# A router in packed float32r products, its logits turned by VectorE and moved by small transfers, and outputs added by transfer

## The chip, the cores and the metric

One core of a Trainium2 chip runs the kernel. The metric is the device time of one execution in microseconds (us). The core's engines work side by side, each through its own queue in order: TensorE (PE; its weight loads are listed as PEld), VectorE (DVE), ScalarE (ACT), GpSimd (POOL) and SyncE (SP), which issues transfers. Queues meet only at semaphores, counters that one instruction raises and another waits for.

## The reference

`x` has 8 x 2048 rows of 256 numbers. It is computed, in float32:

- x = x + attention(layernorm(x)): Q, K, V from 64 x 256 weights, energy = K^T V over each sequence, context = Q energy, out = context Wo^T, all without softmax
- x = x + ffn(layernorm(x)), with h the normalised row:

```
scores = sigmoid(h @ Wr)                      # 8 experts
idx = top 2 of scores + router_bias           # weights are normalised over the two
routed = sum over the 4 MLP experts of cw * (silu(h Wg) * (h Wu)) Wd
       + cw[4] h + cw[6] h + cw[7] relu(h)    # expert 5 gives nothing
shared = causal depthwise convolution of h over 4 rows, plus bias
ffn = routed + shared
```

## The kernel before, in words

The 16384 rows are cut into 32 groups of 512 rows (`GT`, four tiles of 128). The loop runs in steps; in each step every stage works on another group, by the lags of L34: I loads x, L normalises (first layernorm), A transposes it and gathers K^T V, Q projects, X loads x a second time into `acc`, B adds the attention and normalises again, R routes, C runs experts and convolution, Y finishes and stores. A head (`head` of each engine) does groups up to step 7, then `steps(body)` runs steps 7 to 39. The order of each engine's instructions is written out by hand in its `body`. Every fourth step is a chain step (`chain()`): a new sequence starts and the 64 x 64 energy is worked out in short dependent steps. Steps without stage A that are no chain step are drain steps (`drain()`).

Exact products are made from halves: a float32 value is split into a rounded float32r part (`_hi`) and the rest (`_lo`), and three float32r products stand for one (`three`, L408). PE's eight PSUM banks are `ps_gram`, `ps_gu0` to `ps_gu2`, `ps_y0`, `ps_y1`, `ps_sh0`, `ps_sh1`. `ps_sh` holds in turn the transposes of x2 (`x2_transpose`), the router's logits, the attention output, the transposed expert weights and the transposes of xn (`xn_transpose`).

What the change touches, by engine:

- PE, `router` (L535): eight float32 products of a 128 x 128 tile of `x2T` with 128 x 8 router weights, giving logits with token rows on partitions. It waits for the copies `x2T` and for the first `x2T_low`. `weights_transpose` (L593) turns the 128 x 16 expert weights `cw` into `ps_sh1`.
- ACT: `logits_copy` (L867) takes logits and their absolute values out of PSUM, `score_size` and `score_dip` (L888, L894) go on with them, `weights_copy` (L911) takes the transposed weights out.
- DVE: `route_scores` and `route_weights` (L1138, L1160) find the two experts and the weights `cw`; `residual` and `norm2_stats` (L1095, L1103) follow in the queue; `output` (L1215) adds the finished `ps_y` onto `acc`, in two passes; `norm1_stats` (L1083) has a one-element copy (`turn`) between its two parts as a wait.
- POOL: `gate_weight` (L1386) multiplies the gate by the expert weights spread over all partitions (`cwb`); `relu_add` (L1399) is an adding transfer from `x2` to `acc`; `norm2_factors` (L1407) makes scale and shift of the second layernorm for ACT's `norm2` (L834).
- SP, `spread_weights` (L348): stores `cwT` to memory, waits for it, and loads it back four times, spread over the partitions. `body` (L377) has the order load x, store outputs, spread weights, load `acc`.

`gate_up(st, k)` (L414) is a group of six 512-column products, k = 0 to 7; `down(st, stage, e)` (L435) one of twelve 256-column products, e = 0 to 3; `conv_transpose` (L448) puts the convolution into `ps_y`.

## Time and profile before

| what | us |
|---|---|
| median of three runs (lowest, highest) | 886.65 (884.33, 886.78) |
| the profiled execution's own time | 888.19 |
| its span, first to last instruction | 886.4 |
| PE busy in the span | 852.9 (96%) |
| DVE, ACT, POOL busy | 751.2, 643.2, 409.6 |
| mean granted TensorE clock, share of full | 0.988 |

Busy time of PE is modelled up to the end of each product, and products overlap, so the distance between two starts, not the duration, is what a product costs the queue. An idle time stands in brackets with the instruction that ended it. The 1.8 us between span and time lie outside the instructions.

### The profile page before, as it was taken

What the parts mean: (1) busy time and instruction counts of PE and PEld (TensorE: products, weight loads), DVE (VectorE), ACT (ScalarE), POOL (GpSimd) and SP (SyncE); (2) the same over time, 40 slices, a digit from 0 to 9 for tenths busy, and PEclk for the clock granted to TensorE, in tenths of its full rate; (3) what the DMA queues carried; (4) which work ended last, traced back from release to release, by engine and by line L of the source; (5) the groups of instructions that cost most, each with busy time, mean ns of one, the idle gap of its engine ahead of it and who ended that gap; (6) DMA issues with size and microseconds to landing.
All of it is one profiled execution on the core that took longest, in us unless ns stands there. A gap on an engine that the chain in (4) does not pass through costs nothing.

```text
span 886.4 us, 16852 instructions
## 1 busy us (share of the span) xinstructions
PE 852.9 (96%) x5437; PEld 757.1 (85%) x5437; DVE 751.2 (85%) x2093; ACT 643.2 (73%) x1366; POOL 409.6 (46%) x585
## 2 busy tenths in 40 slices
PE   5878999999999999999999999999999999899997
PEld 4667888999889988889899998889988998788886
DVE  4668889988899988999899998999889988678884
ACT  4585867787777777787678777777867875666653
POOL 3214635554455454455355544545535544433332
PEclk9899999999999999999999999999999999999999
DMA  9112354433354442434443344554424344324434
GB/s 286 60 43 54 119 144 138 112 110 100 116 143 143 143 120 67 126 125 138 143 121 104 100 132 120 143 144 126 111 75 131 109 121 119 96 54 118 118 94 119
DMA packets 79447, 103.86 MB, mean 117 GB/s; under 512 B 6528, under 2 KB 58880, under 8 KB 79360
## 3 DMA queue, kind: packets, MB, share of 16 engines
q1 hardware_dynamic: 74752, 86.02, 30.6%
q0 software_dynamic: 4608, 16.78, 10.0%
q8 instruction: 43, 0.70, 0.3%
q14 instruction: 44, 0.36, 0.1%
HBM read 68.96 MB, written 17.04 MB: 97 GB/s over the span
## 4 chain that ended last, share of the span: by engine, by line
PE 77%; DVE 12%; ACT 4%; issue 3%; POOL 2%; DMA 1%; POOLq 0%; DVEq 0%; ACTq 0%
PE ps_gu L410 11%; PE ps_gu L412 10%; PE ps_gu L411 10%; PE ps_sh L541 6%; PE ps_y L410 6%; PE ps_y L411 6%; PE ps_y L412 6%; PE ps_y L460 3%; PE ps_sh L531 3%; PE ps_sh L484 2%; ACT x L842 2%; PE ps_sh L588 1%; PE ps_sh L589 1%; PE ps_gram L618 1%; PE ps_gu L564 1%
## 5 line engine op out<-in xcount | busy, mean ns | idle before, releaser
L1391 POOL TENSOR_TENSOR gate<-gate,cwb 128x512 f32<-128x512 f32 x128 | 168.0, 1313 | 291.4 <-ACT gate L765 265.6
L410 PE MATMUL ps_gu<-x2T_hi,wgu_hi 128*128 128x512 f32 x512 | 211.3, 413 | 1.2 <-DVE hid L1055 1.2
L412 PE MATMUL ps_gu<-x2T_hi,wgu_lo 128*128 128x512 f32 x512 | 202.2, 395 | 0.0
L411 PE MATMUL ps_gu<-x2T_lo,wgu_hi 128*128 128x512 f32 x512 | 201.7, 394 | 0.0
L410 PE MATMUL ps_y<-wd_hi,hid_hi 128*128 128x256 f32 x512 | 153.1, 299 | 2.2 <-DVE hid_lo L1062 2.2
L1073 DVE SCALAR_TENSOR_TENSOR conv<-x2T,conv_w,conv 128x512 f32<-128x512 f32 x192 | 150.6, 822 | 0.0
L411 PE MATMUL ps_y<-wd_lo,hid_hi 128*128 128x256 f32 x512 | 145.4, 284 | 0.0
L412 PE MATMUL ps_y<-wd_hi,hid_lo 128*128 128x256 f32 x512 | 145.0, 283 | 0.0
L1062 DVE TENSOR_TENSOR hid_lo<-hid,hid_hi 128x512 fp32r<-128x512 f32 x101 | 86.2, 853 | 46.2 <-ACT hid_hi L758 46.2
L412 PEld LDWEIGHTS ps_gu<-x2T_hi,wgu_lo 128*128 128x128 f32 x512 | 96.6, 189 | 22.2
L410 PEld LDWEIGHTS ps_gu<-x2T_hi,wgu_hi 128*128 128x128 f32 x512 | 97.2, 190 | 18.4 <-issue 2.3
L411 PEld LDWEIGHTS ps_gu<-x2T_lo,wgu_hi 128*128 128x128 f32 x512 | 97.4, 190 | 13.4
L1055 DVE TENSOR_TENSOR hid<-ps_gu,gate 128x512 f32<-128x512 f32 x128 | 86.2, 673 | 20.8 <-issue 13.3
L410 PEld LDWEIGHTS ps_y<-wd_hi,hid_hi 128*128 128x128 f32 x512 | 97.9, 191 | 4.9 <-DVE hid_lo L1062 3.5
L765 ACT ACTIVATE gate<-ps_gu 128x512 f32<-128x512 f32 x128 | 75.5, 590 | 33.5 <-PE ps_gu L412 32.7
L411 PEld LDWEIGHTS ps_y<-wd_lo,hid_hi 128*128 128x128 f32 x512 | 98.0, 191 | 1.6
L412 PEld LDWEIGHTS ps_y<-wd_hi,hid_lo 128*128 128x128 f32 x512 | 97.5, 190 | 0.0
L758 ACT ACTIVATE hid_hi<-hid 128x512 fp32r<-128x512 f32 x128 | 80.2, 626 | 18.5 <-DVE hid L1055 17.6
L1370 POOL TENSOR_TENSOR mv<-mv,eps_ln 128x4 f32<-128x4 f32 x64 | 24.3, 380 | 136.9 <-DVE mv L1112 114.0
L826 ACT ACTIVATE xn<-xa,shift,rstd 128x256 f32<-128x256 f32 x128 | 66.0, 591 | 6.5 <-POOL shift L1375 6.4
L1373 POOL TENSOR_TENSOR rstd<-mv,half_neg 128x4 f32<-128x4 f32 x64 | 67.4, 1054 | 5.0
L842 ACT ACTIVATE x<-acc,shift,rstd 128x256 f32<-128x256 f32 x128 | 66.3, 593 | 4.3 <-POOL shift L1375 4.2
(126 smaller groups left out, 1877.5 us busy)
## 6 DMA issues: line engine op xcount, KB each, us to landing
cwb<-cw_rows SPq DMA_DIRECT2D x128, 256.0 KB, 4.0
xa<-in_x SPq DMA_DIRECT2D x32, 512.0 KB, 7.8
acc<-in_x SPq DMA_DIRECT2D x32, 512.0 KB, 6.9
acc<-x POOLq DMA_DIRECT2D x32, 512.0 KB, 4.6
out<-acc SPq DMA_DIRECT2D x64, 256.0 KB, 2.6
cwb<-in_wg SPq DMA_DIRECT2D x4, 128.0 KB, 3.9
cwb<-in_wu SPq DMA_DIRECT2D x4, 128.0 KB, 3.7
cwb<-in_wd SPq DMA_DIRECT2D x1, 512.0 KB, 4.5
```

The costliest lines, as they stand in the source:

```text
L410: nc.tensor.matmul(dst, a_hi, b_hi, start=start, stop=False, skip_group_check=True)
L411: nc.tensor.matmul(dst, a_hi, b_lo, start=False, stop=False, skip_group_check=True)
L412: return nc.tensor.matmul(dst, a_lo, b_hi, start=False, stop=stop, skip_group_check=True)
L758: return nc.scalar.activation(dst, src, ACT.Copy, scale=scale)
L765: nc.scalar.activation(gate[:, e % 2], ps_gu[GU_BANK[2 * e]][:, :], ACT.Silu)\
L826: nc.scalar.activation(xn[:, q, t], xa[:, q, t], ACT.Identity, bias=shift1[:, f, t:t + 1], scale=rstd1[:, f, t:t + 1]).then_inc(xn_ready, 1)
L842: nc.scalar.activation(x2[:, q, t], acc[:, st.slot("B", 4), t], ACT.Identity, bias=shift2[:, q, t:t + 1], scale=rstd2[:, q, t:t + 1]).then ...
L1055: v.tensor_tensor(hid[:, e % 2], ps_gu[GU_BANK[2 * e + 1]][:, :], gate[:, e % 2], ALU.mult)\
L1062: v.tensor_tensor(hid_lo[:, k], hid[:, k], hid_hi[:, k].bitcast(F32), ALU.subtract)\
L1073: v.scalar_tensor_tensor(conv[:, c], x2T[:, q, c, k:k + GT], conv_w[:, c, k:k + 1], conv[:, c], ALU.mult, ALU.add).then_inc(conv_ready, 1)
L1373: g.tensor_tensor(rstd, mv[:, :, 1], half_neg[:, :], ALU.pow).then_inc(rstd_ready, 1)
L1391: g.tensor_tensor(gate[:, e % 2], gate[:, e % 2], cwb[:, q, e], ALU.mult).then_inc(gatew_ready, 1)
```

## The change

PE's router becomes four products: the weights are held as 8 columns of high halves, 8 of low halves and 16 of zeros (`wr2`, 128 x 32, float32r), the tokens move past them as 512 columns of `x2T_hi` and then of `x2T_lo`. The logits come out with tokens along the free axis on 32 partitions. DVE turns them in 32 x 32 blocks, POOL adds the two halves of each logit, SP moves them in four transfers to token rows, and ACT takes the absolute value from SBUF. The weights `cw` are turned by DVE instead of PE and ACT, and stored by four transfers. In steps with both Y and C that are no drain steps, ACT copies `ps_y` to `y_rows` and POOL adds it onto `acc` by a transfer. The one-element copy in the first layernorm's statistics goes in the loop. In the head the first group's convolution taps move ahead of the loop; in the last chain step the residual and its statistics go ahead of the routing. The diff, cut to its core:

```diff
+    def by_transfer(self):
+
+        return self.on("Y") and self.on("C") and not self.drain()
...
 # SP
+            def move_logits(st):
+
+                sp.wait_ge(sum_ready, st.before("R", 1, 1))
+                if st.later("R", 1):
+                    sp.wait_ge(cw_ready, st.before("R"))
+                for j in range(P // SQ):
+                    sp.dma_start(logits[j * SQ:(j + 1) * SQ, :], summed[:, j].rearrange("p t e -> p (t e)"))\
+                        .then_inc(logits_loaded, 16)
...
             def spread_weights(st):
-                sp.dma_start(rows.rearrange("a e (t n) -> (a e t) n", t=TG), cwT[:, :]).then_inc(cw_stored, 16)
-                sp.wait_ge(cw_stored, st.before("R", 16, 16))
+                for j in range(P // SQ):
+                    sp.dma_start(rows[:, :, :].rearrange("a e (t n) -> (a e t) n", t=TG)[:, j * SQ:(j + 1) * SQ],
+                                 cwT[j * SQ:j * SQ + EM * TG, :]).then_inc(cw_stored, 16)
+                sp.wait_ge(cw_stored, st.before("R", 64, 64))
...
             def body(st):
                 if st.on("I"):
                     load_x(st)
+                if st.on("R"):
+                    move_logits(st)
                 if st.on("Y"):
...
+                    if st.by_transfer():
+                        sp.wait_ge(y_added, st.before("Y", 16, 16))
...
 # PE: xn_transpose(1) and x2_transpose(1) no longer wait for cwT_ready
             def router(st):
-                pe.wait_ge(x2T_ready, st.before("R", HC, HC))
+                b, q = ps_sh[0][0:SQ, :], st.slot("R", 2)
                 pe.wait_ge(x2Tlo_ready, st.before("R", HC, 1))
-                b, q = ps_sh[0], st.slot("R", 2)
-                for t in range(TG):
-                    for c in range(HC):
-                        last = nc.tensor.matmul(b[:, t * NE:(t + 1) * NE],
-                                                x2T[:, q, c, PAD + t * P:PAD + (t + 1) * P], wr_sb[:, c],
-                                                start=(c == 0), stop=(c == HC - 1))
+                pe.wait_ge(x2Thi_ready, st.before("R", HC, HC))
+                for c in range(HC):
+                    nc.tensor.matmul(b, wr2[:, c], x2T_hi[:, q, c], start=(c == 0), stop=False,
+                                     skip_group_check=True)
+                for c in range(HC):
+                    if c == 1:
+                        pe.wait_ge(x2Tlo_ready, st.before("R", HC, HC))
+                    last = nc.tensor.matmul(b, wr2[:, c], x2T_lo[:, q, c], start=False, stop=(c == HC - 1),
+                                            skip_group_check=True)
                 last.then_inc(router_done, 1)
...
-            def weights_transpose(st):
...
 # ACT
+            def y_copy(st, h):
+
+                if h == 0:
+                    act.wait_ge(y_done, st.before("Y", 1, 1))
+                else:
+                    act.wait_ge(down_done, st.before("Y", EM, EM))
+                if st.later("Y", 1):
+                    act.wait_ge(y_added, st.before("Y", 16))
+                copy(y_rows[:, 2 * h:2 * h + 2].rearrange("p t n -> p (t n)"), ps_y[h][:, :]).then_inc(out_ready, 1)
...
-            def logits_copy(st):
...
             def score_size(st):
-                act.wait_ge(logits_ready, st.before("R", 2, 2))
+                act.wait_ge(logits_loaded, st.before("R", 64, 64))
                 if st.later("R", 1):
                     act.wait_ge(cw_ready, st.before("R"))
+                nc.scalar.activation(size[:, :], logits[:, :], ACT.Abs).then_inc(size_ready, 1)
+                act.wait_ge(size_ready, st.before("R", 1, 1))
...
-            def weights_copy(st):
...
             def head():
                 q_high(at("Q", 1, NG))
-                logits_copy(r)
-                score_size(r)
-                score_dip(r)
                 xnT_head(3, 0)
                 xnT_head(3, 1)
                 q_high(at("Q", 2, NG))
+                score_size(r)
+                score_dip(r)
                 norm1(at("L", 6, NG))
...
             def body(st):   # y_copy(0) follows x2T_out(0), y_copy(1) follows x2T_out(1)
...
                         nc.scalar.activation(a, a, ACT.Identity, bias=skip_bias[:, q, t:t + 1],
                                              scale=skip_scale[:, q, t:t + 1]).then_inc(ident_added, 1)
+                if r_on:
+                    score_size(st)
+                    score_dip(st)
...
 # DVE
+                dve.wait_ge(cw_ready, st.before("R", 1, 1))
+                if st.later("R", 1):
+                    dve.wait_ge(cw_stored, st.before("R", 64))
+                v.transpose(cwT[:, :], cw[:, q].rearrange("p e t -> p (e t)")).then_inc(cwT_ready, 1)
+
+            def logits_turn(st):
+                dve.wait_ge(router_done, st.before("R", 1, 1))
+                if st.later("R", 1):
+                    dve.wait_ge(sum_ready, st.before("R"))
+                v.transpose(turned[:, :, :, :].rearrange("p j t n -> p t j n"),
+                            ps_sh[0][0:SQ, :].rearrange("p (t j n) -> p t j n", t=TG, j=P // SQ))\
+                    .then_inc(turn_ready, 1)
...
                 q_low(at("Q", 3, NG))
+                dve.wait_ge(halo_ready, 1)
+                conv_tap(at("C", 0, NG), 0)
+                conv_tap(at("C", 0, NG), 1, (0,))
                 q_low(at("Q", 4, NG))
                 xnT_low(at("A", 5, NG), 0)
                 xnT_low(at("A", 5, NG), 1)
+                conv_tap(at("C", 0, NG), 1, (1,))
+                conv_tap(at("C", 0, NG), 2, (0,))
...
-                if y_on:
+                if y_on and not st.by_transfer():
                     output(st, 0)
                     output(st, 1)
...
+                if c_on and not first:
+                    hidden(st, 0)
+                if r_on:
+                    logits_turn(st)
+                if c_on and not first:
                     conv_tap(st, 2)
...
                     hidden(st, 2)
+                if b_on and m_on and not st.on("A"):
+                    residual(st, 0)
+                    residual(st, 1)
+                    norm2_stats(st)
                 if r_on:
                     route_scores(st)
...
 # POOL
+            def y_add(st):
+
+                k = st.slot("Y", 4)
+                pool.wait_ge(relu_added[st.slot("Y", 2)], st.uses("Y", 2, 16, 16))
+                pool.wait_ge(out_ready, st.before("Y", 2, 2))
+                g.dma_start(acc[:, k].rearrange("p t n -> p (t n)"), y_rows[:, :, :].rearrange("p t n -> p (t n)"),
+                            accum_op=ALU.add).then_inc(y_added, 16)
...
+            def logits_sum(st):
+
+                pool.wait_ge(turn_ready, st.before("R", 1, 1))
+                if st.later("R", 1):
+                    pool.wait_ge(logits_loaded, st.before("R", 64))
+                g.tensor_tensor(summed[:, :, :, :].rearrange("p j t e -> p (j t) e"),
+                                turned[:, :, :, 0:NE].rearrange("p j t e -> p (j t) e"),
+                                turned[:, :, :, NE:2 * NE].rearrange("p j t e -> p (j t) e"), ALU.add)\
+                    .then_inc(sum_ready, 1)
...
                 norm2_factors(at("B", 1, NG))
+                logits_sum(at("R", 0, NG))
...
                     gate_weight(st, 1)
+                if r_on:
+                    logits_sum(st)
+                if st.by_transfer():
+                    y_add(st)
                 if c_on:
                     gate_weight(st, 2)
```

## Rows read from the trace of the kernel before

**Rows 1.** Windows: us; busy us of PE, PEld, DVE, ACT, POOL; clock; DMA.

```profile
124.37:749.15 624.78, 623.97 (x4082) 558.88 (x4081) 559.68 (x1549) 480.54 (x1023) 316.46 (x428) 1.00 0.42 120
404.27:429.39 25.12, 25.12 (x166) 22.78 (x165) 22.81 (x66) 19.65 (x42) 13.35 (x19) 1.00 0.43 127
429.39:458.30 28.91, 28.87 (x189) 25.21 (x188) 25.26 (x68) 21.50 (x49) 13.19 (x19) 1.00 0.38 114
```

**Rows 2.** Timeline of PE around one router: start us, duration us, engine, line.

```profile
409.15 1.84 PE L541 MATMUL ps_sh<-wr_sb,x2T 128*128 128x8 f32 x16
410.86 0.48 PE L410 MATMUL ps_gu<-x2T_hi,wgu_hi 128*128 128x512 f32 x1
411.18 0.39 PE L411 MATMUL ps_gu<-x2T_lo,wgu_hi 128*128 128x512 f32 x1
411.41 0.39 PE L412 MATMUL ps_gu<-x2T_hi,wgu_lo 128*128 128x512 f32 x1
```

**Rows 3.** Timeline of PE at the transpose of the expert weights.

```profile
425.40 0.27 PE L600 MATMUL ps_sh<-ident,cw 128*16 128x128 f32 x1
425.51 0.60 PE L484 MATMUL ps_sh<-ident,xn 128*128 128x128 f32 x4
```

**Rows 4.** Timelines: the round from x2's transposes to the next x2.

```profile
405.46 0.60 PE L531 MATMUL ps_sh<-ident,x 128*128 128x128 f32 x4
417.64 0.40 PE L412 MATMUL ps_gu<-x2T_hi,wgu_lo 128*128 128x512 f32 x1
418.13 0.69 DVE L1055 TENSOR_TENSOR hid<-ps_gu,gate 128x512 f32<-128x512 f32 x1 [0.51 <-issue]
422.50 0.22 DVE L1179 TENSOR_TENSOR cw<-raw,winv 128x32 f32<-128x32 f32 x1
428.11 0.20 POOL L1375 TENSOR_TENSOR shift<-negm,rstd 128x4 f32<-128x4 f32 x1
428.64 2.07 ACT L842 ACTIVATE x<-acc,shift,rstd 128x256 f32<-128x256 f32 x4
```

**Rows 5.** Timelines: what stands before and behind the router.

```profile
409.34 0.67 DVE L1186 TENSOR_TENSOR x2T_lo<-ps_sh,x2T_hi 128x512 fp32r<-128x512 f32 x1
407.96 0.60 ACT L758 ACTIVATE x2T<-ps_sh 128x512 f32<-128x512 f32 x1 [0.78 <-PE ps_sh L531]
413.70 1.03 PE L460 MATMUL ps_y<-ident,conv 128*128 128x128 f32 x8
414.91 2.07 ACT L1005 ACTIVATE acc<-acc,skip_bias,skip_scale 128x256 f32<-128x256 f32 x4
```

**Rows 6.** Group (busy us, mean ns, idle before); transfers (KB, us to landing); SP's timeline.

```profile
L1186 DVE TENSOR_TENSOR x2T_lo<-ps_sh,x2T_hi 128x512 fp32r<-128x512 f32 x64 | 42.9, 671 | 15.0 <-ACT x2T_hi L758 14.3
cw_rows<-cwT SPq DMA_DIRECT2D x32, 8.0 KB, 1.4
acc<-x POOLq DMA_DIRECT2D x32, 512.0 KB, 4.6
acc<-in_x SPq DMA_DIRECT2D x32, 512.0 KB, 6.9
400.88 0.33 SPq L353 DMA_DIRECT2D cw_rows<-cwT  x1
```

**Rows 7.** Timelines of DVE and POOL where both work on SBUF at once.

```profile
415.05 1.44 DVE L1062 TENSOR_TENSOR hid_lo<-hid,hid_hi 128x512 fp32r<-128x512 f32 x1 [0.72 <-ACT hid_hi L758]
414.64 1.30 POOL L1391 TENSOR_TENSOR gate<-gate,cwb 128x512 f32<-128x512 f32 x1 [3.27 <-ACT gate L765]
```

**Rows 8.** Timelines of the head, the first expert step and the first drain step.

```profile
52.33 2.08 ACT L826 ACTIVATE xn<-xa,shift,rstd 128x256 f32<-128x256 f32 x4
53.53 0.20 POOL L1375 TENSOR_TENSOR shift<-negm,rstd 128x4 f32<-128x4 f32 x1
74.69 1.62 PE L460 MATMUL ps_y<-ident,conv 128*128 128x128 f32 x8 [2.91 <-DVE conv L1073]
771.66 1.86 PE L531 MATMUL ps_sh<-ident,x 128*128 128x128 f32 x4 [2.16 <-ACT x L842]
```

More of the change, by code:

```diff
@@ L398, in _ @@
             load_x(at("I", 7, NG))
+            move_logits(at("R", 0, NG))
             spread_weights(at("R", 0, NG))
@@ L740, in body @@
                     gram_halves(st)
-                if drain:
-                    down(st, "C", 2)
-                if r_on:
-                    weights_transpose(st)
                 if a_on and r_on:
                     xn_transpose(st, 0)
-                if c_on and not drain:
+                if c_on:
                     down(st, "C", 2)
@@ L865, in f_copy @@
                            [(f1[:, :], ps_gram[:, 0:H]), (f2[0:D, :], ps_gram[0:D, 0:H])], fhi_out)
-            def logits_copy(st):
-                act.wait_ge(router_done, st.before("R", 1, 1))
-                if st.later("R", 1):
-                    act.wait_ge(cw_ready, st.before("R"))
-                copy(logits[:, :], ps_sh[0][:, 0:TG * NE]).then_inc(logits_ready, 1)
-                nc.scalar.activation(size[:, :], ps_sh[0][:, 0:TG * NE], ACT.Abs).then_inc(logits_ready, 1)
             def halo(st):
@@ L909, in conv_begin @@
                         .then_inc(tap_ready, 1)
-            def weights_copy(st):
-                act.wait_ge(cwT_done, st.before("R", 1, 1))
-                if st.later("R", 1):
-                    act.wait_ge(cw_stored, st.before("R", 16))
-                copy(cwT[:, :], ps_sh[1][0:EM * TG, 0:P]).then_inc(cwT_ready, 1)
             def xnT_head(n, c):
@@ L974, in body @@
                     x2T_out(st, 0)
+                if st.by_transfer():
+                    y_copy(st, 0)
                 if m_on:
@@ L978, in body @@
                     x2T_out(st, 1)
+                if st.by_transfer():
+                    y_copy(st, 1)
                 if m_on:
@@ L1019, in body @@
                     norm1(st)
-                if r_on:
-                    weights_copy(st)
-                if st.on("B") and st.drain():
+                if st.on("B") and not st.on("A"):
                     norm2(st)
@@ L1031, in body @@
                     xnT_high(st, 1)
-                if st.on("B") and not st.drain():
+                if st.on("B") and st.on("A"):
                     norm2(st)
@@ L1060, in hid_low @@
                 dve.wait_ge(hidhi_ready, st.before("C", EM, e + 1))
+                if e == 0 and st.on("L") and not st.later("C", 1):
+                    dve.wait_ge(stat1, st.before("L", TG, TG))
                 k = e % 2
@@ L1063, in hid_low, with conv_tap @@
                     .then_inc(hidlo_ready[k], 1)
-            def conv_tap(st, n):
+            def conv_tap(st, n, parts=range(HC)):
                 q, k = st.slot("C", 2), PAD - 1 - n
-                for c in range(HC):
+                for c in parts:
                     if n == 0:
@@ L1090, in norm1_stats, with norm1_aggr, norm1_both @@
                     v.bn_stats(stats1[:, f, t], xa[:, q, t]).then_inc(stat1, 1)
-                turn(stat1, st.before("L", TG, TG))
+            def norm1_aggr(st):
+                f = st.slot("L", 2)
                 for t in range(TG):
                     v.bn_aggr(mv1[:, f, t], stats1[:, f, t]).then_inc(aggr1, 1)
+            def norm1_both(st):
+                norm1_stats(st)
+                turn(stat1, st.before("L", TG, TG))
+                norm1_aggr(st)
             def residual(st, h):
@@ L1185, in x2T_low @@
                 dve.wait_ge(x2Thi_ready, st.before("R", HC, c + 1))
+                if c == 0 and st.on("L") and st.later("C", 1):
+                    dve.wait_ge(stat1, st.before("L", TG, TG))
                 v.tensor_tensor(x2T_lo[:, q, c], ps_sh[c][:, :], x2T_hi[:, q, c].bitcast(F32), ALU.subtract)\
@@ L1267, in head @@
                 q_low(at("Q", 1, NG))
+                logits_turn(r)
                 residual(at("B", 1, NG), 0)
@@ L1329, in body @@
                     hid_low(st, 2)
-                if b_on and not drain:
+                if b_on and st.on("A"):
                     residual(st, 0)
```

99 lines of the change are left out of this document (53 added, 46 removed).

## The prediction

> **What bounds the kernel now.** I read the windows first, then PE's timeline in one step, then the other engines' timelines beside it. In the six rounds of four steps between the chain steps' routers, PE is busy 623.97 of 624.78 us at granted clock 1.00, that is at 2.4 GHz [rows 1]. A plain step takes 25.12 us with PE busy in all of it, DVE in 22.81, ACT in 19.65; the longer window of a chain step, 28.91 us, is as full [rows 1]. Busy time of PE is modelled, so I looked at starts: 512-column products of one kind start 0.23 us apart with nothing between [rows 2]. PE's queue is therefore the price list: what leaves it shortens the step until another wait ends last.
>
> The next limit is near. The round from one x2 to the next is closed: x2_transpose(0) at 405.46, gate_up(5)'s last product ends at 417.64 + 0.40 = 418.04, DVE's hidden(2) starts at 418.13, the routing gives cw at 422.50, then residual and statistics, POOL's shift is ready at 428.31, ACT's pass over x2 runs from 428.64 to 430.71 [rows 4]. PE comes to the next x2_transpose(0) one step of 25.12 [rows 1] after 405.46, at 430.58: it starts before the last of four ACT passes has ended. No slack is left there.
>
> **Router (PE).** From its start at 409.15 to the next group's at 410.86 it takes 1.71 us. The first product after it needs 0.32 us instead of 0.23 [rows 2]; I charge the 0.09 to the change from float32 to float32r. Removed: 1.80. Added: four float32r products of 512 columns. The trace has none with a 128 x 32 weight tile; the nearest rows, with 128 x 128, stand 0.23 apart, and I take that, since a smaller tile has less to load: 4 x 0.23 = 0.92. The dear end is 4 x 0.32 = 1.28. Net: -0.88, at worst -0.52. The fourth product waits for x2T_low(1), which ended at 410.01 [rows 5]; PE would be there at 409.15 + 0.69 = 409.84. With 0.35 us won ahead of it on DVE (the statistics' second half moves behind x2T_low(0), the one-element copy goes) the wait is 0 to 0.2 us.
>
> **Weights' transpose (PE).** Its slot runs from 425.40 to 425.51 [rows 3]: -0.11. ACT loses the copy behind it and the waits of xn_transpose(1) go. Together PE alone would save 0.99 us per step: 24.13 instead of 25.12.
>
> **DVE.** Two output passes on a PSUM bank go, 2 x 0.67 by [rows 6], x2T_low, the nearest pass of that size; logits_turn comes, 32 x 512 from PSUM, between 0.22 (cw, 128 x 32 [rows 4]) and the port-slowed 1.44 [rows 7]; I take 0.67, since the free size is the same 512. cw's transpose costs a wait of 0.1 and about 0.2 by the cw row, 0.3 in all, at most 0.67. The sum is -0.4, but the 0.3 lies on the closed round and the output passes did not. That round becomes 12.58 (405.46 to 418.04) - 0.88 + 0.09 + 12.58 (418.13 to 430.71) + 0.3 - 0.2 - 0.13 = 24.34. The 0.2 is ACT's: its pass began 0.33 after POOL's shift because its queue was full, and the lost copy and an earlier q_high free it. The 0.13 is the overlap of PE's first transposes with the last pass. So the step is 24.34, and PE waits about 0.2 us in it: **-0.8 per step**. x2's ACT pass is what is late next.
>
> **ACT.** The copies of ps_y are 2 x 0.60. The first fits the 0.78 us for which ACT waits between the two x2T_out [rows 5]; the second pushes silu(1), gate_weight(1) and hidden(1) by some 0.3, which DVE does not notice as its queue is behind. Without that gap, up to 1.2 us of 5.47 idle (25.12 - 19.65) go. conv_transpose waits for y_copy instead of output, and y_copy is earlier.
>
> **POOL and SP.** logits_sum stands ahead of gate_weight(2), and y_add too; the cover is the 3.27 us for which POOL waits there [rows 7]. The sum costs 0.20 (128x4, [rows 4]) to 1.30 (128x512, [rows 7]), taken 0.5, since 128 elements a lane are nearer to 4; y_add costs an issue. Its landing takes 4.6 us [rows 6]. SP waits for it ahead of the store of cw, which comes only after the routing, about 12 us later: covered. On SP, move_logits issues four transfers ahead of the outputs and spread_weights three more stores; at 0.33 each [rows 6] that is 1.3 us each time. The store of this step was issued at 400.88 + 25.12 = 426.00 [rows 1, 6], 3.3 after cw was there at 422.72, since PE's and ACT's part lay between; now it begins at 423.0, and the last of four at 424.0, so the spread weights come some 2 us sooner.
>
> **Do the logits arrive in time?** In the step of [rows 5]: router ends 410.2, hidden(0), turn to 411.4, sum to 411.9, four issues to 413.2, landing 1.4 [rows 6] after the last issue began: 414.3. ACT asks for them after its skip passes, 416.98 less the step's 0.8 [rows 5]: slack 1.9. DVE needs the result at 418.7, and ACT's three small passes end some 0.8 after the skip: about 1 us of further slack.
>
> **Steady part.** 25 router intervals from step 8 to 33 x 0.8 = 20.0 us. Chain steps are as full of PE [rows 1] and have the same router and round; I use the same 0.8.
>
> **Head.** logits_sum stands behind norm2_factors, whose shift is ready at 53.73 [rows 8]. Sum 0.5, issues 1.3, landing 1.4: 56.9, the three small passes to 57.7. ACT's queue holds norm1 behind them, which started at 52.33 [rows 8]: 5.3 late, and everything up to step 7's x2_transpose hangs on ACT there; cw's transpose adds 0.3. Gained: the 2.91 us that PE waited for the convolution taps, and the slower products after it (eight transposes 1.62 against 1.03 [rows 5, 8], the twelve of down(0) by about 1.0, an estimate in the same ratio): 1.6. Net **+1.0**, between -3 and +4.
>
> **End.** In the last chain step the residual moves ahead of the routing: of the 2.16 us wait [rows 8] and the slow products after it most goes, but hid_low(2) now stands behind more: -2.5, between 0 and -4. Three drain steps at -0.8: -2.4. The last store of cw has no cover; it loses PE's and ACT's part and gains three issues: 0.
>
> **Sum:** -20.0 + 1.0 - 2.5 - 2.4 = -23.9. The profiled execution took 888.19 with a span of 886.4; it would be 864.3 with 862.5. The median, 1.54 lower, would be about **863**.
>
> **The rivals.**
>
> A, the gain is given back at the port of DVE and POOL. While POOL's gate ran, DVE's hid_low took 1.44 us [rows 7] instead of 0.67 as x2T_low [rows 6]. logits_sum falls on conv_tap(2), and conv_transpose (413.70 [rows 5]) would come at 413.0 with the taps done at 412.6: 0.4 of slack. A sum of 1.30 instead of 0.5, or y_add's issue held back, costs 0.4 to 0.8 a step: half of the gain goes, 25 x 0.4 = 10 more, 873; at 0.8 all of the steady gain, 883. For it: DVE's and POOL's like overlaps are in every step. Against: the sum is small. The Trainium skill (SBUF — State Buffer, SBUF: two separate sides) says that such a pair of operations takes the shared port by turns, the loser waiting for the whole instruction; the 1.44 agrees. By that rule alone one sum costs DVE no more than its own 0.5, 0.1 beyond the slack: 25 x 0.1 = 2.5, near 865.
>
> B, slower: the logits are late. Place: ACT's score_size, in front of relu, conv_begin, silu(3). Price: every us past the slacks goes into the step. With landing L, a step changes by -0.8 + max(0, L - 1.4 - 2.4), my 2.4 lying between ACT's 1.9 and DVE's 2.9; it is slower from 4.6 on. At 6.9, the landing of acc<-in_x [rows 6], +2.3: 25 x 2.3 = 58, with head and end (-3.9) about 940. At 5.0 it is +0.4, 893. Against it: that row moves 512 KB, these 4 KB in a transfer, and the small store's is 1.4.
>
> C, the change doesn't do what it says: the 32-wide product costs more than a 128-wide one, or other waits than PE's end the step. Then the router stays at 1.3 to 1.8 us, the step gains 0 to 0.4, and with head and end the time is 873 to 883.
>
> **How the numbers follow.** Forecast (PE-bound or nearly, -0.6 to -0.99 a step) 0.70, A 0.14, B 0.06, C 0.10. About 0.3%, 2.7 us, is what a measurement of this kernel can tell from no change. Of A and C, 0.04 lies within that; B is slower but for the cases below 4.6, and I add 0.01 for a head that is stuck longer. Faster 0.89, same 0.04, slower 0.07. The forecast's own range: -0.99 x 28 and the good ends of head and end (-3, -4) give 852; -0.6 x 28 with +4 and 0 give 874. The range that holds 8 in 10 is **852 to 876**: it takes in A's nearer half and C's best, and leaves out the rest of A and C, and B.
>
> **What would show it.** The router's four products at 0.23 us spacing, 24.2 to 24.5 us from router to router in plain steps, no PE slot between gram_halves and xn_transpose; PE's waits, some 0.2 us a step, put down to ACT's x pass. DVE's turn at 0.6 to 0.7 us, POOL's sum under 0.7, ACT's abs without a wait for the transfer. In the head ACT idle for some 4 us ahead of the abs, but no wait of PE for conv taps in step 7. Wrong would be: PE waiting for conv, hid_lo or q in each plain step; ACT waiting for the logits in the loop; router products 0.3 us apart or more; DVE without any idle time in a step; or a head longer by over 4 us.

## The result: 930.6 us, 5% slower

The changed kernel took 930.62 us (median of 4 runs, 930.25 to 931.7) against 885.49 for the kernel before in the same runs: ratio 1.0499, 95% interval 1.0478 to 1.0521. The forecast was 863, range 852 to 876. The profiled execution has a span of 928.8 us, 42.4 more than before.

The page's first line, then two windows (us; busy us of PE, PEld, DVE, ACT, POOL; clock; DMA share; GB/s): one plain step, and the same six rounds of four steps as in [rows 1], from chain router to chain router:

```profile
PE 839.3 (90%) x5021; PEld 709.6 (76%) x5021; DVE 760.8 (82%) x2081; ACT 661.4 (71%) x1355; POOL 487.0 (52%) x644
```

```profile
404.27:430.95 26.68, 24.80 (x152) 21.12 (x152) 23.80 (x66) 20.43 (x41) 16.35 (x21) 1.00 0.55 139
129.01:791.47 662.46, 616.43 (x3770) 524.45 (x3768) 566.52 (x1526) 499.05 (x1023) 384.38 (x476) 0.99 0.52 133
```

A plain step takes 26.68 us instead of 25.12, and PE, busy in all of it before, now has idle time, 1.9 us in the step and 46.0 us in the six rounds (0.8 before). From the first router to the last the trace is 42.10 us longer: the two intervals at the head +3.43 (forecast +1.0), the next 25 together +38.98 (691.20 against 652.22), which is 1.56 each (forecast -20.0), the last chain step -1.63 (forecast -2.5), the three drains +1.32 (forecast -2.4). TensorE's clock is a small part of it: three chain intervals hold a stretch of 3.4 us at granted clock 0.50 and take 30.99, 31.19 and 31.83 us, the two next to them without one 30.91 and 30.80, so some 1.5 us in all.

Four of the rows on what waits for what in the whole changed kernel (us in total, times, longest):

```profile
ACT size L911 <- DMA logits<-summed: 58.8, 27, 5.4
PE ps_sh L515 <- DVE acc L1121: 35.2, 23, 3.2
DVE rmag L1162 <- ACT mag L913: 27.7, 20, 2.8
PEld ps_sh L574 <- DVE x2T_lo L1219: 18.9, 23, 1.5
```

The first row is a wait that the kernel before cannot have, as ACT copied the logits from PSUM itself. One plain step, by the engines' timelines (start us, duration us, engine, line, operation, tiles, in brackets the idle time before and who ended it):

```profile
404.87 0.70 DVE L1210 STREAM_TRANSPOSE turned<-ps_sh 32x512 f32<-32x512 f32 x1
405.50 1.36 DVE L1086 SCALAR_TENSOR_TENSOR conv<-x2T,conv_w,conv 128x512 f32<-128x512 f32 x2
406.79 0.67 DVE L1075 TENSOR_TENSOR hid_lo<-hid,hid_hi 128x512 fp32r<-128x512 f32 x1
...
411.83 0.69 DVE L1066 TENSOR_TENSOR hid<-ps_gu,gate 128x512 f32<-128x512 f32 x1 [0.15 <-issue]
413.52 0.35 DVE L1162 RECIPROCAL rmag<-mag 128x32 f32<-128x32 f32 x1 [1.00 <-ACT mag L913]
...
417.21 0.21 DVE L1204 STREAM_TRANSPOSE cwT<-cw 128x32 f32<-128x32 f32 x1
417.80 1.43 DVE L1075 TENSOR_TENSOR hid_lo<-hid,hid_hi 128x512 fp32r<-128x512 f32 x1 [0.38 <-ACT hid_hi L773]
```

```profile
405.65 2.14 POOL L1488 TENSOR_TENSOR summed<-turned 32x128 f32<-32x128 f32 x1 [0.15 <-DVE turned L1210]
407.74 0.92 POOL L1470 DMA_DIRECT2D acc<-y_rows  x1
...
417.39 1.29 POOL L1449 TENSOR_TENSOR gate<-gate,cwb 128x512 f32<-128x512 f32 x1 [4.28 <-ACT gate L780]
```

```profile
407.81 3.33 SPq L368 DMA_DIRECT2D logits<-summed  x4
...
417.45 1.72 SPq L377 DMA_DIRECT2D cw_rows<-cwT  x4
420.20 2.90 SPq L386 DMA_DIRECT2D cwb<-cw_rows  x4
```

```profile
412.91 0.23 ACT L911 ACTIVATE size<-logits 128x32 f32<-128x32 f32 x1 [2.20 <-DMA logits<-summed]
...
424.30 2.08 ACT L869 ACTIVATE x<-acc,shift,rstd 128x256 f32<-128x256 f32 x4 [0.23 <-POOL shift L1433]
```

PE's router of the next step, beside [rows 2]:

```profile
429.88 0.61 PE L569 MATMUL ps_sh<-x2T_hi,wr 128*32 128x512 f32 x2
430.33 0.40 PE L574 MATMUL ps_sh<-x2T_lo,wr 128*32 128x512 f32 x1
431.08 0.42 PE L574 MATMUL ps_sh<-x2T_lo,wr 128*32 128x512 f32 x1 [0.35 <-DVE x2T_lo L1219]
```

From the turn's end at 405.57 it is 2.22 us to the end of POOL's sum, and from there, through four issues and their landings, 5.12 us until ACT has the logits: 7.3. The forecast had 3.2 there (0.5, then 1.3 and 1.4). Of the 4.1 beyond that, ACT shows 2.20 as waiting (it was ready at 410.71) and VectorE's routing 1.00. The routing stands in front of hid_low(2) and the residual on VectorE, the residual in front of x2 and of PE's xn_transpose(0): hence the 35.2 us of PE waiting for acc. Counted on the closed round of [rows 4]: from hidden(2)'s start at 411.83 to the end of ACT's pass over x2 at 426.38 it is 14.55 us, where it was 12.58. In it are 1.00 of waiting for mag, 0.38 of waiting for hid_hi(2), which ACT made late, and 0.76 because hid_low(2) now falls on POOL's gate_weight(3) and takes 1.43 instead of 0.67.

### The profile page after: what moved, and what is told of

Read it like the earlier page. It is cut to its first block and busy times, and to the rows that moved or that the text cites. A ratio compares the mean times of both kernels' runs of the same rounds, so it can differ in the third digit from the quotient of the medians.

```text
span 928.8 us, 16330 instructions
## 1 busy us (share of the span) xinstructions
PE 839.3 (90%) x5021; PEld 709.6 (76%) x5021; DVE 760.8 (82%) x2081; ACT 661.4 (71%) x1355; POOL 487.0 (52%) x644
## 5 line engine op out<-in xcount | busy, mean ns | idle before, releaser
L1449 POOL TENSOR_TENSOR gate<-gate,cwb 128x512 f32<-128x512 f32 x128 | 171.6, 1341 | 255.2 <-ACT gate L780 230.6
L441 PE MATMUL ps_gu<-x2T_hi,wgu_hi 128*128 128x512 f32 x512 | 209.1, 408 | 3.4 <-DVE hid L1066 3.4
L1075 DVE TENSOR_TENSOR hid_lo<-hid,hid_hi 128x512 fp32r<-128x512 f32 x101 | 111.4, 1103 | 44.0 <-ACT hid_hi L773 43.7
L1428 POOL TENSOR_TENSOR mv<-mv,eps_ln 128x4 f32<-128x4 f32 x64 | 30.3, 473 | 114.0 <-DVE mv L1132 91.2
L869 ACT ACTIVATE x<-acc,shift,rstd 128x256 f32<-128x256 f32 x128 | 66.5, 590 | 19.5 <-issue 13.8
```

The source lines that it names most:

```text
L441: nc.tensor.matmul(dst, a_hi, b_hi, start=start, stop=False, skip_group_check=True)
L869: nc.scalar.activation(x2[:, q, t], acc[:, st.slot("B", 4), t], ACT.Identity, bias=shift2[:, q, t:t + 1], scale=rstd2[:, q, t:t + 1]).then ...
L1075: v.tensor_tensor(hid_lo[:, k], hid[:, k], hid_hi[:, k].bitcast(F32), ALU.subtract)\
L1449: g.tensor_tensor(gate[:, e % 2], gate[:, e % 2], cwb[:, q, e], ALU.mult).then_inc(gatew_ready, 1)
```

## The experiments

Theory 1 is the account above: the logits' lateness sets the step. Theory 2: the y transfer does it, through GpSimd's and SP's queues. Theory 3: the new order on VectorE and ScalarE does it, whatever the logits. Times, and ratios to the kernel before in the same runs with their 95% intervals (three rounds each, five for the last):

| run | us | ratio |
|---|---|---|
| e5 before, with the y transfer | 888.45 | 1.0018 [0.9993, 1.0043] |
| e1 y on VectorE | 909.86 | 1.0257 [1.0209, 1.0305] |
| e2 sum on VectorE | 887.80 | 1.0012 [0.9988, 1.0036] |
| e8 both on VectorE | 904.26 | 1.0207 [1.0189, 1.0226] |
| e6 y_add later | 899.41 | 1.0147 [1.0127, 1.0168] |
| e13 sum later | 897.89 | 1.0144 [1.0127, 1.0161] |
| e7 score later | 949.56 | 1.0725 [1.0709, 1.0741] |
| e3 pieces on VectorE | 903.19 | 1.0180 [1.0132, 1.0227] |
| e15 pieces on GpSimd | 889.82 | 1.0044 [1.0026, 1.0061] |
| e9 low between the taps | 892.07 | 1.0072 [1.0053, 1.0092] |
| e10 and the turn of cw later | 897.50 | 1.0130 [1.0106, 1.0154] |
| e12 pieces later | 880.94 | 0.9952 [0.9938, 0.9967] |
| e14 GpSimd pieces later | 909.39 | 1.0267 [1.0242, 1.0291] |
| e16 gate first | 902.87 | 1.0199 [1.0172, 1.0226] |

### The y transfer and the sum

e5, the kernel before with y_copy, y_add and SP's wait for y_added as in the diff:

> The kernel before with the y transfer alone: ScalarE copies ps_y, GpSimd issues an accumulating transfer, SP waits for it ahead of the output's stores and the store of cw; router, logits and weights' transpose as before. Theory 1: VectorE loses 1.34 us a step, ScalarE gains 1.2 of which 0.78 fits a gap; PE sets the step at 25.1 with or without it: 880 to 892. Theory 2: 15 us or more slower than before, 900 or more.

888.45, no measurable difference, as theory 1 had it. Alone the transfer does no harm. e1, the changed kernel without it:

```
 def by_transfer(self):
-    return self.on("Y") and self.on("C") and not self.drain()
+    return False
```

> The changed kernel with the output added by VectorE from the PSUM banks, as before, and no y transfer; the new router and its way to token rows stay. If the late logits cost the time (theory 1), ScalarE still waits for them at the same place, and VectorE takes 2 x 0.67 us more per step: 925 to 940, ACT's wait for the logits still 1.5 us or more in a plain step. If the y transfer costs it by holding GpSimd's queue and slowing SP's issues and landings (theory 2): the four logits issues fall from 3.3 to about 1.5 us, the wait goes, and the time is 885 or below.

909.86, between the two. ACT's wait for the logits fell to 7.7 us, against theory 1's number. All links of the way to ACT got shorter. The transfers of 4 KB (KB each, median us from issue to landing; first row e1, then the changed kernel):

```profile
logits<-summed SPq DMA_DIRECT2D x128, 4.0 KB, 1.7
```

```profile
logits<-summed SPq DMA_DIRECT2D x128, 4.0 KB, 3.2
```

Four issues took 2.42 us in e1 instead of 3.33. And the sum took 0.95 us in a plain step instead of 2.13: the output passes stand ahead of the turn on VectorE, and GpSimd waits for it:

```profile
397.73 0.95 POOL L1488 TENSOR_TENSOR summed<-turned 32x128 f32<-32x128 f32 x1 [1.74 <-DVE turned L1210]
```

So this run alone does not say what the y transfer costs the logits; e6 below does. With the output passes back on VectorE the taps are late, and PE waits for those in 20 steps:

```profile
PEld ps_y L491 <- DVE conv L1086: 19.8, 21, 1.0
...
PE ps_y L491 <- DVE conv L1086: 10.7, 20, 0.5
```

e2 moves the sum to VectorE, right behind logits_turn, and off GpSimd's list:

```
...
+                v.tensor_tensor(summed[:, :, :, :].rearrange("p j t e -> p (j t) e"),
+                                turned[:, :, :, 0:NE].rearrange("p j t e -> p (j t) e"),
+                                turned[:, :, :, NE:2 * NE].rearrange("p j t e -> p (j t) e"), ALU.add)\
+                    .then_inc(sum_ready, 1)
```

> The changed kernel with the sum of the logits' two halves on VectorE right behind the turn, not on GpSimd; the four transfers stay. Left of GpSimd's part is its wait and its 2.13 us; VectorE pays 0.2 to 0.3. Theory 1: the logits come some 1.8 us sooner, and since each us of their lateness goes into the step (26.7 against 24.3 forecast), 28 steps gain up to 1.8 each: 880 to 890. Theory 2 (the y transfer): no more than 5 us gained, 925 to 931. Theory 3 (the new order of VectorE and ScalarE, apart from the logits, costs the time): 920 or more too, and then e3 tells nothing better.

887.80, inside theory 1's range. The sum takes 0.28 us there, ACT waits 5.8 us for the logits in the whole run, and the plain step is 25.04. Theories 2 and 3 fall as sole causes. e8 is the fourth corner, both edits:

> The fourth corner: sum of the logits on VectorE and the output on VectorE too (no y transfer); the packed router, the turn, the four transfers and the weights' turn stay. If the two causes of late logits are one account (each alone was enough to bring them in time), this gains little against the run with the sum on VectorE (887.8): VectorE has 1.34 us more per step, its taps stand behind that, and PE waits for conv as in the run with the output on VectorE: 895 to 908. If they add up independently (-43 and -21): 867.

904.26: not additive. With the sum on GpSimd the y transfer costs 20.8 us (930.6 against 909.9), with the sum on VectorE it gains 16.5 (887.8 against 904.3). The two edits bring the logits in time by the same account, and only the transfer keeps VectorE's taps in time.

e6 asks what in the y transfer delays the logits. y_add is issued one place later:

```
-                if st.by_transfer():
-                    y_add(st)
                 if c_on:
                     gate_weight(st, 2)
+                    if st.by_transfer():
+                        y_add(st)
```

> The changed kernel with GpSimd's y_add issued one place later, behind gate_weight(2) instead of ahead of it, so that the logits' four small transfers start before the 512 KB accumulating transfer and not with it. The sum stays on GpSimd. If the logits' issue (3.3 us for four) and landing (3.2 us) are slow because that transfer is under way (with the y transfer gone altogether they were 2.4 and 1.7), they fall to these values, the logits come some 2.4 us sooner, ACT's waits for them fall from 58.8 us to under 15, and 28 steps gain 1.2 to 1.7 each: 882 to 897. If issue and landing have another cause, the wait stays at 50 us or more and the time at 925 to 932.

Four issues took 2.41 us again, the landing was 1.7, and the time 899.41; ACT's wait fell to 24.7, not under 15: the sum still takes its 2.13 us. From the first issue until ACT has the logits it is 3.61 us in a plain step (393.52 to 397.13), 5.10 in the changed kernel (407.81 to 412.91). So 1.5 of the 4.1 us come from y_add, which GpSimd issues 0.07 us ahead of the first of the four there. That the 512 KB transfer is under way is not enough: in e13, below, the four come 2.3 to 3.6 us behind y_add, which lands after 4.6, and are nearly as fast as alone; in e2 they come 0.5 behind it and are slow (3.2 us for four, landing 3.3), but in time. Which part of a start so close together does it is not shown. The Trainium skill (DMA: Bandwidth & Descriptors, Issuing engines are not separate DMA queues) says that transfers started by different engines run on the same 16 DMA engines and interleave, and that the time to initiate one is usually small beside the transfer. The landings of 1.7 and 3.2 us fit the first in part, since e13's landed in 1.9 beside the large one; as to the second, one issue here takes 0.59 us (median) of a landing of 1.7, and four stand in a row.

### The price of lateness, and its way

e13: as e2, with the one sum behind hid_low(0).

> A price for lateness by itself: the run with the sum on VectorE (887.8), with the sum's one instruction moved behind conv_tap(2) and hid_low(0). The same work on the same engines; the logits leave about 2.0 us later and nothing else waits for them but the transfers. ACT waited 5.8 us in all there, so the slack is about 0.3. If lateness alone is the cost, some 24 steps grow by 1.4 to 1.7: 920 to 930, with ACT's wait for the logits at 45 us or more. If it was GpSimd's occupied queue that cost the time in the changed kernel, this stays at 885 to 895.

897.89: a gain lost of 10 us where 32 to 42 were expected. The issues came 2.3 to 3.6 us behind y_add's and were fast again (median 2.55 us for four, landing 1.9). From the first issue to the last landing it is 3.7 us in most plain steps, 4.7 in e2, so half of the 2.0 us was given back: ACT's wait is 19.5 us. Four runs differ mainly in when the logits come, besides who makes the sum and where y_add stands (e2, e13, e6 and the changed kernel: waits 5.8, 19.5, 24.7, 58.8 us; times 887.8, 897.9, 899.4, 930.6). From end to end the time grows by 42.8 us for 53.0 us of ACT's wait, 0.81 for each; between neighbours it is 0.3 to 0.9, so this is no fixed price.

e7 moves ACT's three passes and the relu behind conv_begin, silu(3) and hid_high(2), sum and transfer as in the change:

```
...
                     silu(st, 3)
                     hid_high(st, 2)
+                if late:
+                    score_relu()      # score_size, score_dip, the four relu passes
```

> The changed kernel, POOL sum and y transfer as they are, with ScalarE's three small passes on the logits and the relu moved behind conv_begin, silu(3) and hid_high(2). The logits come as late as before; what changes is who stands behind them. If their lateness goes into the step through ScalarE's queue (rival B's place), the step loses most of its 1.7 us of excess over a plain step of the run with the sum on VectorE: 890 to 905. If it goes through VectorE's routing, ahead of hid_low(2) and the residual (the price of 1.9 plus 1.0 of slack that I took from there), it stays at 920 to 935.

949.56, worse than either number. ACT no longer waits for the logits, and VectorE waits for ACT instead (the changed kernel: 27.7):

```profile
DVE rmag L1168 <- ACT mag L913: 71.4, 26, 2.8
```

Rival B had put the place in front of ACT's relu, conv_begin and silu(3). With conv_begin, silu(3) and hid_high(2) ahead of the late passes nothing was gained, so VectorE's routing is a place too, and a dear one. But the edit also starts the passes later than the logits allow (in one plain step at 397.81, with the last landing at 396.07), so it does not split the changed kernel's cost between the two. The split is read from the step above: 1.00 us of VectorE's routing waiting for mag, 0.38 through ACT's late hid_high(2).

### No transfer of the logits at all

e3: VectorE adds in four pieces that write straight to the 32-row blocks, right behind the turn.

```
+                for j in range(P // SQ):
+                    v.tensor_tensor(logits[j * SQ:(j + 1) * SQ, :].rearrange("p (t e) -> p t e", t=TG),
+                                    turned[:, j, :, 0:NE], turned[:, j, :, NE:2 * NE], ALU.add)
```

> The changed kernel with the sum on VectorE in four pieces of 32 rows that write straight to the 32-row blocks of the logits: no GpSimd sum and no logits transfer. VectorE pays four small operations, estimated 0.2 each. Theory 1: the logits are ready about 1 us after the turn, some 6.5 us sooner than in the changed kernel, ACT never waits for them, and the time is what I forecast for the rest: PE-bound steps of 24.3 to 24.7, 858 to 872. Theories 2 and 3: 915 or more, because the y transfer and the order stay.

903.19: the worst miss of this study. The logits are in time, but four pieces of 183 ns, 1.15 us with their gaps, stand in front of conv_tap(2), and PE waits for conv:

```profile
L488 PEld LDWEIGHTS ps_y<-ident,conv 128*128 128x128 f32 x256 | 28.0, 141 | 20.1 <-DVE conv L1083 19.0
```

e15 has the same four pieces on GpSimd, at the sum's old place:

> The changed kernel with the sum still on GpSimd and at its old place, but in four pieces of 32 rows that write straight into the logits' token rows (each waits for the one before): no logits transfer. GpSimd stays occupied there as long as before or longer, 2 to 3 us, beside conv_tap(2). If only the arrival of the logits counts, they are there at about 408.5 of the plain step whose ScalarE asks for them at 410.7: no wait, and the time is near that of the sum on VectorE, 880 to 892. If GpSimd's occupied port or queue is the cost, it stays above 905.

889.82, as theory 1 said. The pieces in a plain step, and a row on waits in the whole run (us in total, times, longest):

```profile
413.07 2.90 POOL L1490 TENSOR_TENSOR logits<-turned 32x32 f32<-32x32 f32 x4 [0.18 <-DVE turned L1207]
DVE hid L1063 <- POOL gate L1446: 28.9, 23, 1.6
```

GpSimd is occupied there longer than before (2.90 us for the four, beside the taps, where the sum took 2.13); only the arrival has changed. So nearly all of the loss of 45 us is the logits' lateness, not what GpSimd does. That is not free either: VectorE waits 28.9 us for gate_weight behind the pieces, 6.7 in the changed kernel, and the plain step is 25.4 us, not the 25.04 of e2.

### What ends the step once the logits are in time

e2's step is 25.04 us, not the 24.34 of the forecast. In its step hidden(2) starts at 468.73 and ACT's pass over x2 ends at 481.63, 12.90 us (forecast 12.55); the rest of the round is 12.14 (forecast 11.79). DVE, POOL, SP and PE in it:

```profile
472.76 0.92 DVE L1198 TENSOR_TENSOR cw<-raw,winv 128x32 f32<-128x32 f32 x1
473.71 0.21 DVE L1204 STREAM_TRANSPOSE cwT<-cw 128x32 f32<-128x32 f32 x1
473.85 0.65 DVE L1075 TENSOR_TENSOR hid_lo<-hid,hid_hi 128x512 fp32r<-128x512 f32 x1
```

```profile
472.31 1.30 POOL L1456 TENSOR_TENSOR gate<-gate,cwb 128x512 f32<-128x512 f32 x1 [2.61 <-ACT gate L780]
```

```profile
461.30 0.42 PE L574 MATMUL ps_sh<-x2T_lo,wr 128*32 128x512 f32 x1 [0.33 <-DVE x2T_lo L1226]
```

cw, 0.22 in [rows 4], ends with gate_weight(3), 0.70 late. In the kernel before the gate fell on another operation of the routing instead, raw, which took 0.52 there and 0.19 in e2, so the net loss is 0.37. The router's last product waits 0.33 for x2T_low(1) by the row. Counted from start to start it comes 0.74 behind the third instead of 0.23, 0.5 late. e9 takes that wait away by putting x2T_low(1) between the two operations of conv_tap(1); e10 also moves cw's transpose behind the residual:

```
-                    conv_tap(st, 1)
+                    conv_tap(st, 1, (0,))
                 if r_on and not first:
                     x2T_low(st, 1)
+                if c_on and not first:
+                    conv_tap(st, 1, (1,))
```

> Sum on VectorE as in the run that took 887.8, and besides x2T_low(1) between the two operations of conv_tap(1) instead of behind both. PE's wait for x2T_low(1) inside the router (0.33 us in a plain step) should go, as ACT's x2T_hi(1) is there 0.6 us before. If the closed round from x2 to x2 sets the step, it gains up to 0.33 in some 24 steps: 879 to 884. If other waits end the step, it stays at 886 to 889.

> As the run with x2T_low(1) between the taps, and the transpose of cw moved on VectorE from ahead of hid_low(2) and the residual to behind the residual, with its wait: 0.35 us less on the closed round, but the stores of cw start some 1.9 us later. Closed round sets the step: another 0.3 a step, 870 to 877. If the spread weights come too late then (GpSimd's gate_weight(0) waits for them, 1 us or more in plain steps, and hidden(0) behind it): no gain or a loss, 880 to 900.

Both lost: 892.07 and 897.50. In e9 the wait for x2T_low went (0.2 us left in all) and one for conv came, since the sum, the turn and the taps share one queue; in e10 GpSimd waits for the spread weights in 29 steps, where it was 10 in e2 (first row e9, second e10):

```profile
PE ps_y L491 <- DVE conv L1086: 6.3, 20, 0.6
POOL gate L1466 <- DMA cwb<-cw_rows: 47.0, 29, 5.7
```

e12 combines what fell into place: VectorE's four pieces, so no transfer, but the turn and the pieces behind hidden(1), where VectorE waited 0.70 us for ACT, and x2T_low(1) between the taps (which come 1.0 us sooner without the turn ahead of them).

```
...
                     hidden(st, 1)
+                if r_on and late:
+                    logits_turn(st)
+                if r_on and not first:
+                    logits_rows(st)        # the four pieces
...
```

> A version meant to be faster: logits added in four pieces straight into token rows by VectorE (no transfer for them), but turn and pieces behind hidden(1), where VectorE waited 0.70 us for ACT, so that the taps come 1.0 us sooner; x2T_low(1) between the taps of conv_tap(1); in the drain the old places. The y transfer stays. If the closed round sets the step once the logits are in time, it loses PE's 0.33 us wait for x2T_low(1) without the wait for conv_transpose that took its place: 24.4 to 24.8 in a plain step, 868 to 880. If cw's collision with GpSimd's gate_weight(3) or the spread weights end the step anyway: 884 to 892.

880.94, just above the expected range, 0.5% faster than the kernel before. Plain steps are 24.66 us, and the router's four products take 0.92 us of PE's queue there, as forecast. The window of one, and three of VectorE's rows in another:

```profile
406.56:431.23 24.67, 24.13 (x155) 20.95 (x155) 23.57 (x68) 20.71 (x43) 13.79 (x19) 1.00 0.57 146
```

```profile
504.37 2.02 DVE L1083 SCALAR_TENSOR_TENSOR conv<-x2T,conv_w,conv 128x512 f32<-128x512 f32 x2
...
511.31 1.85 DVE L1083 SCALAR_TENSOR_TENSOR conv<-x2T,conv_w,conv 128x512 f32<-128x512 f32 x2
...
521.96 0.78 DVE L1195 TENSOR_TENSOR cw<-raw,winv 128x32 f32<-128x32 f32 x1
```

VectorE is busy in 23.57 of 24.67 us, and between 504.37 and 529.03 its timeline names no wait. Its two pairs of taps take 0.6 and 0.5 more than the 1.39 of the pair at 408.02 in the kernel before, cw 0.56 more than in [rows 4]. The closed round is 11.89 and 12.77 us there (506.04 to 517.93, and to 530.70), near the forecast's 11.79 and 12.55. So VectorE looked like the last bound, and e14 takes the four pieces from it: GpSimd does them, the turn stands behind hid_low(0).

> The four GpSimd pieces and no logits transfer, with the turn moved on VectorE behind hid_low(0) and x2T_low(1) between the taps of conv_tap(1). In the run of 880.9 VectorE had no idle time left in a plain step of 24.66 us, 1.15 us of it the four pieces. If VectorE is what ends that step, this one takes 24.2 to 24.5 and 868 to 877. If the pieces on GpSimd collide with VectorE's passes on SBUF, or push gate_weight(2) and hidden(2), it gives that back: 880 to 895.

909.39: on GpSimd the pieces and y_add's issue now stood ahead of gate_weight(2), and VectorE's hidden(2) waited 1.2 us in a plain step. e16 puts gate_weight(2) first, and in the head the pieces ahead of norm2_factors:

> The run with GpSimd's pieces placed later took 909 because on GpSimd the pieces and y_add's issue stood ahead of gate_weight(2): hidden(2) waited 1.19 us for it in a plain step of 25.9. Here gate_weight(2) goes ahead of both, and in the head the pieces go ahead of norm2_factors. If that order was the cause, hidden(2) waits under 0.3 us, ScalarE finds the logits in time (at 481.8 of a step in which it asked at 482.6), and the step falls to that of the run of 880.9 or below it, 24.2 to 24.7: 866 to 880, the head 1 to 3 us of it. If GpSimd's work beside VectorE is the bound (hid_low(1), xn_low and the routing collide with gate_weight(2), the pieces and gate_weight(3)), it stays at 885 or above.

902.87, its second case. A plain step, VectorE and GpSimd:

```profile
482.32 1.43 DVE L1072 TENSOR_TENSOR hid_lo<-hid,hid_hi 128x512 fp32r<-128x512 f32 x1 [0.38 <-ACT hid_hi L770]
...
503.53 0.35 DVE L1159 RECIPROCAL rmag<-mag 128x32 f32<-128x32 f32 x1 [0.32 <-ACT mag L910]
```

```profile
481.91 1.29 POOL L1451 TENSOR_TENSOR gate<-gate,cwb 128x512 f32<-128x512 f32 x1 [1.48 <-ACT gate L777]
...
500.47 2.41 POOL L1495 TENSOR_TENSOR logits<-turned 32x32 f32<-32x32 f32 x4 [0.17 <-POOL gate L1451]
```

The pieces take 2.41 us beside hid_low(1) and xn_low, the logits are late again (VectorE waits 0.32 for mag), and hid_low(2) collides with gate_weight(3) as in the changed kernel. Its head gained: the two first intervals are 49.05 us together, 51.77 in e14, where the pieces stand behind norm2_factors. Whether 24.3 can be had with a further order is open; I found none.

## Why the prediction was wrong

**What held.** The router's products stand 0.23 us apart, and where nothing is late the four take 0.92 us (e12). So rival C's first half, the dear product, fell. The turn took 0.70 (0.67 taken), cw's transpose 0.21 and its wait 0.1 (0.3 in all). The closed round was the right frame, and x2's ACT pass is what is late next: x2's first four transposes take 0.74 us of PE's queue in e2 and 0.83 in e12, where they took 0.36. The wait for conv in the first expert step went.

**The step that failed: "Do the logits arrive in time?"** Its three terms were all too small. (1) "The sum costs 0.20 to 1.30, taken 0.5": it took 2.13 us (median), outside the range, and 2.22 with the start. I read collisions as costing VectorE and wrote the sum's 1.30 into rival A; I never asked what the collision costs the sum and carried that into the landing. (2) "At 0.33 each that is 1.3": four issues took 3.3 us, 2.4 undisturbed. The 0.33 was one store's, and it was no bound for a row of four. (3) "landing 1.4 after the last issue began": a median of 3.2 right behind y_add, 1.7 without. I had y_add "cost an issue" and looked only at who waits for it, not at what it does to the transfers that start beside it. Together 7.3 us against 3.2, with a slack of 2.9. Of the 4.1 us too much, the sum with its start has 1.7, issues and landing even undisturbed 0.9 (3.6 for 2.7), and y_add beside them 1.5.

**Rival A** had the port, but on the wrong side: at conv_tap(2) the sum lost there, not VectorE, whose pair took 1.36 us. VectorE lost at hid_low, 1103 ns on average instead of 853, 25 us over the run. **Rival B** was the mechanism, with a chance of 0.06. Its price per step, -0.8 + max(0, L - 3.8), gives +0.9 with L = 1.4 + 4.1; measured +1.56. Of the rest, 0.34 is in the first half of the round (12.13 against the 11.79 of the forecast); the second half also has hid_low(2), which lateness pushed onto gate_weight(3) (0.76). Its place was half right: besides ACT's queue it is VectorE's routing. **Rival C's second half**, that other waits than PE's end the step, came true behind B: the router stood at some 1.45 us in plain steps, as its last product came 0.5 late behind x2T_low(1), where I had allowed 0 to 0.2.

**"-0.8 per step" would have failed too.** With the logits in time (e2) the 25 steady intervals are 0.4 us longer than before in sum, not 20.0 shorter. A plain step is 25.04, a gain of 0.08 and not 0.8. Half of the 0.7 missing there is x2T_low(1)'s wait in the first half of the round (12.14 against 11.79), half cw's collision with gate_weight(3) in the second (12.90 against 12.55). I had taken cw at its undisturbed 0.22; POOL's gate, moved with everything else, now fell on it, and on raw no longer:

```profile
421.50 0.52 DVE L1167 SCALAR_TENSOR_TENSOR raw<-marked,score 128x32 f32<-128x32 f32 x1
```

**The spread weights** "come some 2 us sooner": from cw's end to the next issue it was 4.66 us before (422.72 to 427.38) and is 3.03 in the changed kernel (417.17 to 420.20). There the stores begin 1.2 us ahead of relu_add's issue. In e2 they begin 0.4 us behind it (473.95 against 473.55), run beside that 512 KB transfer, and the same stretch is 5.35 us (473.68 to 479.03), dearer than before. e10, which began the stores later still, had no room there.

**Head**: forecast +1.0, measured +3.4. logits_sum behind norm2_factors is dearer than reckoned: ACT waited 5.39 us for the logits and norm1 started at 58.57, 6.2 later than in [rows 8] (forecast 5.3). While PE waited 7.51 us for q there, its granted clock fell to 0.5 (1.2 GHz) and stayed there for 10.2 us; the two first intervals have a mean of 0.87, 0.93 before. The forecast had no term for that. With the sum on VectorE (e2, 0.97) the head is 1.3 us shorter than before. **End**: of the last chain step's -2.5 came -1.63; the drains lost 0.4 each instead of gaining 0.8.

## What to carry to other kernels

Price a hand-over by every link in it, each at its disturbed duration: the operation that makes the data, the issues in a row, the landing beside whatever transfer starts with it, and set the sum against the slack of the tightest reader on any engine, not of the first. When a step is bound by a closed round and the engines beside it are nearly full (here VectorE 91%, ScalarE 78% of a plain step), a gain on one is worth only what the next collision leaves; try the order before you count the saving. Where data fits 32-row blocks, as here, an engine that writes them in place can be sooner than transfers (1.15 us for four pieces on VectorE, 3.6 to 5.1 for the four transfers), provided its pieces stand where that engine waits anyway (e12 against e3, 22 us, with x2T_low(1) moved besides).

## What was not expected of the hardware

A GpSimd operation with a VectorE queue of two-SBUF-input operations beside it seems to lose more than one turn. The sum took 0.44 us at the least. In the loop it started 0.15 us behind the start of conv_tap(2)'s pair; it took 1.53 us where hid_low(0) came 1.2 us behind that pair (chain step, 130.95), and 2.13 where hid_low(0) followed at once, ending 0.3 us behind hid_low(0). Where GpSimd had been waiting 0.77 us or more for the turn, it took 0.95 (in e1, with 0.86 us or more, 0.95 to 0.97), and the pair of taps came out longer, 1.64 instead of 1.36. Why the wait before makes this difference is not shown:

```profile
103.31 0.95 POOL L1488 TENSOR_TENSOR summed<-turned 32x128 f32<-32x128 f32 x1 [0.77 <-DVE turned L1210]
130.95 1.53 POOL L1488 TENSOR_TENSOR summed<-turned 32x128 f32<-32x128 f32 x1 [0.17 <-DVE turned L1210]
432.31 2.13 POOL L1488 TENSOR_TENSOR summed<-turned 32x128 f32<-32x128 f32 x1 [0.16 <-DVE turned L1210]
```

The Trainium skill (SBUF — State Buffer, SBUF: two separate sides) has the loser wait for the winner's whole instruction; the 0.95 agrees, for one instruction. The 2.13 would be three in a row for which the loser stands back: it ends 0.3 us behind the third, as the 1.53 ends 0.3 behind the second. The long span is no artefact of the profile: y_add, next on GpSimd, starts at 407.74 and SP's first issue, which waits for the sum, at 407.81, where the sum of 405.65 ends.
